# New order lists for an attention and LoRA block on one core, and the small vectors on SyncE's queue

## What is computed

```python
x = x + attn(layernorm(x))      # 32 query heads, 8 key/value heads of 128, q and k rms-normed, ALiBi, causal
x = x + ffn(layernorm(x))       # 8 LoRA experts of rank 16, all used, weighted by a softmax router
# attn: q, k, v = x@Wq.T, x@Wk.T, x@Wv.T;  out = softmax(q k^T/sqrt(128) + bias) v;  out @ Wo.T
# ffn:  2 * sum_h 8*softmax(x@Wr.T + br)_h * (x @ A_h.T) @ B_h.T
```

## Time and profile before

| | us |
|---|---|
| median of 3 runs | 2099.63 (2098.99 to 2102.61) |
| the profiled execution | 2102.15 |
| its span, first to last instruction | 2100.4 |
| PE busy in it | 2031.2 (97%) |
| DVE, ACT, POOL busy | 1364.3, 1149.8, 1113.1 |

### The profile page before, as it was taken

How to read it: one execution, slowest core, us unless ns; L and a number is a source line. 1 busy time by engine, 2 the same in 40 slices (tenths; PEclk the granted TensorE clock), 3 DMA queues, 4 the chain that set the end, 5 groups by cost and what they waited for, 6 DMA issues and landing times.

```text
span 2100.4 us, 33654 instructions
## 1 busy us (share of the span) xinstructions
PE 2031.2 (97%) x11196; PEld 1724.8 (82%) x11196; DVE 1364.3 (65%) x3431; ACT 1149.8 (55%) x3314; POOL 1113.1 (53%) x1128
## 2 busy tenths in 40 slices
PE   7999999999999999999999999999999999999996
PEld 6888888888888888887878788887888888787874
DVE  6657656566666666669765666565666656566785
ACT  4656546565555646655545455555555555555551
POOL 3554645546355554646645656454564645456462
PEclk9999999999999999999999999999999999999998
DMA  3573535636364463654544536354453635444342
GB/s 121 145 166 89 150 95 150 141 105 156 102 162 100 127 171 85 159 160 130 133 125 115 126 81 148 95 125 116 106 107 90 146 94 127 117 104 98 80 99 64
DMA packets 738699, 252.35 MB, mean 120 GB/s; under 512 B 551000, under 2 KB 682072, under 8 KB 738528
## 3 DMA queue, kind: packets, MB, share of 16 engines
q1 hardware_dynamic: 686192, 147.96, 33.4%
q10 hardware_dynamic: 52336, 102.25, 14.1%
HBM read 136.86 MB, written 113.25 MB: 119 GB/s over the span
## 4 chain that ended last, share of the span: by engine, by line
PE 87%; DVE 5%; ACT 2%; POOL 2%; issue 2%; DMA 1%; SPq 0%; ACTq 0%; DVEq 0%; POOLq 0%
PE s_ps L1047 18%; PE o_ps L1047 17%; PE y_ps L1047 16%; PE q_ps L1047 15%; PE turn_ps L1134 11%; PE turn_ps L1047 8%; POOL pT_lo L826 1%; DVE oT_lo L970 1%; ACT pT_hi L735 1%; ACT oT_hi L762 1%; PE turn_ps L1128 1%; DVE pT_lo L919 1%; DMA p_raw<-p_bounce 0%; DVE qn L953 0%; SPq L589 0%
## 5 line engine op out<-in xcount | busy, mean ns | idle before, releaser
L826 POOL TENSOR_TENSOR pT_lo<-p_raw,pT_hi 128x512 fp32r<-128x512 f32 x256 | 331.1, 1300 | 243.2 <-ACT pT_hi L735 242.7
L820 POOL TENSOR_TENSOR probs_odd<-probs_odd,p_inv 128x256 f32<-128x256 f32 (+3 forms) x256 | 316.5, 1256 | 186.1 <-DVE p_inv L949 185.9
L820 POOL TENSOR_TENSOR probs_even<-probs_even,p_inv 128x128 f32<-128x128 f32 (+3 forms) x256 | 261.1, 1042 | 196.6 <-DVE p_inv L949 195.6
L735 ACT ACTIVATE pT_hi<-p_raw 128x512 fp32r<-128x512 f32 x256 | 161.4, 631 | 238.3 <-PE o_ps L1047 132.5
L919 DVE TENSOR_TENSOR pT_lo<-turn_ps,pT_hi 128x512 fp32r<-128x512 f32 x320 | 218.1, 684 | 93.8 <-ACT pT_hi L727 92.4
L1047 PE MATMUL s_ps<-kT_hi,qT_hi 128*128 128x512 f32 (+3 forms) x768 | 273.2, 356 | 3.5 <-DVE neg_max L942 2.2
L942 DVE CUSTOM_DVE_ANT_0 probs_odd<-s_ps,rel 128x256 f32<-128x256 f32 (+3 forms) x256 | 209.0, 820 | 98.9 <-issue 97.6
L727 ACT ACTIVATE pT_hi<-turn_ps 128x512 fp32r<-128x512 f32 x320 | 188.8, 596 | 150.5 <-PE turn_ps L1134 148.8
L1047 PE MATMUL s_ps<-kT_hi,qT_lo 128*128 128x512 f32 (+3 forms) x768 | 262.3, 341 | 0.0
L1047 PE MATMUL s_ps<-kT_lo,qT_hi 128*128 128x512 f32 (+3 forms) x768 | 261.4, 340 | 0.0
L1047 PE MATMUL o_ps<-pT_hi,v_hi 128*128 128x512 f32 x576 | 244.2, 424 | 13.7 <-POOL pT_lo L826 8.1
(11 more groups left out here) (110 smaller groups left out, 4614.3 us busy)
## 6 DMA issues: line engine op xcount, KB each, us to landing
p_raw<-p_bounce SPq DMA_DIRECT2D x1024, 64.0 KB, 2.3
p_bounce<-probs_odd SPq DMA_DIRECT2D x64, 320.0 KB, 2.8
p_bounce<-probs_odd SPq DMA_DIRECT2D x64, 192.0 KB, 4.2
p_bounce<-probs_even SPq DMA_DIRECT2D x64, 192.0 KB, 2.1
wq_kept<-wqT_hi ACTq DMA_DIRECT2D x8, 1024.0 KB, 4.4
wq_kept<-wqT_lo ACTq DMA_DIRECT2D x8, 1024.0 KB, 6.8
p_bounce<-probs_odd SPq DMA_DIRECT2D x64, 128.0 KB, 1.8
p_bounce<-probs_even SPq DMA_DIRECT2D x64, 128.0 KB, 1.8
```

Source lines behind the costliest of these rows:

```text
L735: nc.scalar.activation(pT_hi[:, p_slot[w, s, j], :], p_raw[:, fetch_number[w, s, j] % RAW_TILES, :], ACT.Copy).then_inc(sems["upper_p"], 1)
L820: nc.gpsimd.tensor_tensor(row, row, p_inv[:, s % 2, h:h + 1].to_broadcast((P, L)), ALU.mult).then_inc(sems["normalise"], 1)
L826: nc.gpsimd.tensor_tensor(pT_lo[:, r, :], p_raw[:, fetch_number[w, s, j] % RAW_TILES, :], pT_hi[:, r, :].bitcast(F32), ALU.subtract).then_ ...
```

## The change

The three small loads are taken from the front of ACT's program and put into SP's, in `load_wo.first`, ahead of its wait. Every string has a new order; each has exactly the items that it had (125, 498, 666, 503, 465 and 569). The tables `MEMORY_TILES`, `MEMORY_SLOTS` and `RAW_TILES` can now differ from batch to batch, but both batches have the values of before; the counting of slots and raw tiles starts anew with the second batch.

```diff
-MEMORY_TILES = {2: (2,), 3: (2, 3), 4: (3, 4), 5: (3, 4, 5), 6: (4, 5, 6), 7: (3, 4, 5, 6, 7)}
+MEMORY_TILES = ({2: (2,), 3: (2, 3), 4: (3, 4), 5: (3, 4, 5), 6: (4, 5, 6), 7: (3, 4, 5, 6, 7)},
+                {2: (2,), 3: (2, 3), 4: (3, 4), 5: (3, 4, 5), 6: (4, 5, 6), 7: (3, 4, 5, 6, 7)})
-    TURN_SLOTS, MEMORY_SLOTS, RAW_TILES = 2, 2, 3
+    TURN_SLOTS = 2
+    MEMORY_SLOTS, RAW_TILES = (2, 2), (3, 3)
 @@ block.sync, load_wo(w, *first)
+                    sp.dma_start(wk_norm[:], k_norm_w.rearrange("(p a) -> p a", a=1)).then_inc(small_loaded, 16)
+                    sp.dma_start(wq_norm[:], q_norm_w.rearrange("(p a) -> p a", a=1)).then_inc(small_loaded, 16)
+                    sp.dma_start(br_row[:], br.rearrange("(a n) -> a n", a=1).broadcast_to((P, NE))).then_inc(small_loaded, 16)
                     after(sp, "turn", "wq", 0, C - 1)
                     sp.dma_start(w_raw[:, 0:G, :], wo_v[0]).then_inc(wo_loaded, 16)
 @@ block.scalar
-            act.dma_start(wk_norm[:], k_norm_w.rearrange("(p a) -> p a", a=1)).then_inc(small_loaded, 16)
-            act.dma_start(wq_norm[:], q_norm_w.rearrange("(p a) -> p a", a=1)).then_inc(small_loaded, 16)
-            act.dma_start(br_row[:], br.rearrange("(a n) -> a n", a=1).broadcast_to((P, NE))).then_inc(small_loaded, 16)
```

The strings, cut to the parts that the text below speaks of. PROLOGUE (its head; what follows has a new order too):

```diff
-"load_y.0 load_y.4 load_wq.first x_stats.0 x_moments.0 x_stats.4 load_y.3 x_moments.4 load_y.2 x_rstd.4 load_y.7 "
-"x_rstd.0 x_norm.4 load_y.1 x_norm.0 turn.wq.0 load_y.5 turn.wq.1 x_stats.3 high.wq.0 turn.wq.2 load_wkv.first "
+"load_y.0 load_y.1 load_y.4 load_wkv.first x_stats.0 load_y.3 x_moments.0 x_stats.1 x_rstd.0 load_y.5 x_moments.1 "
+"x_stats.4 load_wq.first x_rstd.1 x_norm.1 turn.wkv.0 x_norm.0 high.wkv.0 x_stats.3 turn.x.0 x_stats.5 turn.x.1 "
+"load_y.7 high.x.0 x_moments.4 low.wkv.0 high.x.1 x_rstd.4 load_y.2 x_moments.3 low.x.0 x_rstd.3 turn.wkv.1 "
+"load_y.6 low.x.1 high.wkv.1 x_moments.5 x_norm.3 turn.wq.0 low.wkv.1 turn.wq.1 high.wq.0 high.wq.1 low.wq.0 "
+"turn.wq.2 low.wq.1 high.wq.2 turn.wq.3 x_stats.2 turn.kv.0 high.wq.3 load_wo.first low.wq.2 x_moments.2 low.wq.3 "
```

More of the change, by code:

```diff
@@ L330, in attention_lora_block, with through_memory, values_order @@
         plans.setdefault(w, group_a if w < NG else group_b)
-    def through_memory(s):
-        return list(MEMORY_TILES.get(s, ()))
-    def values_order(s):
-        return [j for j in range(s + 1) if j not in through_memory(s)] + through_memory(s)
+    def through_memory(w, s):
+        return list(MEMORY_TILES[w // NG].get(s, ()))
+    def values_order(w, s):
+        return [j for j in range(s + 1) if j not in through_memory(w, s)] + through_memory(w, s)
     def ffn_batch(w):
@@ L484, in attention_lora_block, with p_high, p_low, raw_p @@
         b_sorted = f_x[:, 1, :].rearrange("p (o h r) -> p o h r", o=C, r=RK)
+        def p_high(slot):
+            more = slot - TURN_SLOTS - MEMORY_SLOTS[0]
+            return pT_hi[:, slot, :] if more < 0 else w_raw[:, 2 * more, :].bitcast(F32R)
+        def p_low(slot):
+            more = slot - TURN_SLOTS - MEMORY_SLOTS[0]
+            return pT_lo[:, slot, :] if more < 0 else w_raw[:, 2 * more + 1, :].bitcast(F32R)
+        def raw_p(n):
+            return p_raw[:, n, :] if n < RAW_TILES[0] else w_raw[:, G + n - RAW_TILES[0], :]
         def x_source(b, t):
@@ L571, in send_p @@
             def send_p(w, s, h):
-                first = through_memory(s)[0]
+                first = through_memory(w, s)[0]
                 before = [name for name in sent if name[1] % 2 == s % 2 and sent[name] == sent[w, s] - 16 * G]
                 if before and h == 0:
-                    after(sp, "flip_p", *before[0], through_memory(before[0][1])[-1])
+                    after(sp, "flip_p", *before[0], through_memory(*before[0])[-1])
                 after(sp, "normalise", w, s, h)
@@ L896, in low @@
                     r = p_slot[w, *which]
-                    target, upper = pT_lo[:, r, :], pT_hi[:, r, :]
+                    target, upper = p_low(r), p_high(r)
                 elif of == "q":
```

66 lines of the change are left out of this document (36 added, 30 removed), and 512 rows, old and new, of tables (BOUNDARY, FIRST_B, GROUP_A, GROUP_B).

## The result

The changed kernel takes 2083.03 us in the median of four runs (2082.91 to 2086.43), the kernel before 2100.53 beside it (2098.99 to 2102.61). The ratio is 0.9915, with a 95% interval of 0.9902 to 0.9929. That is 17.5 us less, where 7.0 was forecast. Measured once more, the changed kernel took 2084.90 and the kernel before 2101.36 beside it, a ratio of 0.9919 (0.9905 to 0.9932). The traced execution of the changed kernel took 2086.43, 3.3 us more than its other three; none of those three has a trace.

What follows compares the result with a forecast made beforehand. PE, busy 97% of the span, bounds the kernel; only 69 us idle can go. Terms -1.5 -1.4 -1.0 -0.8 +0.9 -3.2 sum to -7.0; with the profiled run's offset to the median carried over, 2092.6 us, range 2085 to 2102.

Steps and rivals of the forecast that it cites:

- GROUP_A: Seven groups of the first batch: net -0.2 us a group, -1.4 in all, each off by 0.4 either way.
- GROUP_B: Six groups of the second batch: net +0.15 us a group, +0.9 in all, with +0.68 ahead of `y.7`.
- Prologue: Start of the kernel: PE starts at 7.5, Wq lands near 12; 1.5 us gained, bounds 3 gained to 1.5 lost.
- Rival (4): Small loads on SP's queue: moving them saves issue time only, prologue starts at 8.0, not 7.5; no chance of its own.
- so the first wait goes: End of a first-batch group: PE's 0.48 us wait for `lower_p.7.7` goes, as `q.9.2` adds 0.68 of work before `values.7.7`.
- BOUNDARY: Group between the batches: +0.7 at its start, -1.7 of its 4.7 idle by judgement; net -1 us, from -3 to +2.
- FIRST_B: First group of the second batch: `lower_p` waits go in large part, `y.6` being ahead of `values.7.6`; -0.8 us, -2.5 to +1.5.
- rival (1): Gains given back, 2100 us: a `low` or `max` moved behind a `flip_p` waits for its DMA; chance 0.25.
- LAST: Last group: +0.9 at its start, -0.6 in the middle, -3.5 at its end; net -3.2 us, from -7 to +3.
- a chain ... 18.05 us: Last group: from `y.6` through `add_y.6`, norm, `turn.f.6`, gates and `turn.lora.6` to `f_out.6`, 18.05 us.
- (2): Slower, 2106 us: `load_wkv` beside tile fetches makes `values.7.6` and `values.7.7` late by 1.9 in seven groups; chance 0.12.
- (3): Larger gain, 2087 us: the list's slack is better throughout, steady groups at -0.6 and -0.3 us each; chance 0.2.

Runs made afterwards that it cites:

- The joints: Kernel before, BOUNDARY in the new order only behind `y.3`, only up to `f_out.1`, or only up to `f_out.3`: 2106.93, 2099.97 and 2097.60 us.

## Why the prediction was wrong

The direction was right. The size was not: the range's lower end was 2085, and the kernel took 2083. The terms of GROUP_A and GROUP_B came out within 0.5 us, the first of them by luck.

- **Bound and method.** PE's work stayed as it was and only idle time went, as said, but for some half-clock time. The step that failed in the method is "An order changes a stall in one way: by how much PE work lies between". An order also moves what stands in DVE's and POOL's queues: `norm_k` beside `lower_p.7.7`, `o_low.6` behind a flip, the fetches of FIRST_B 2.4 us late. The chain's length is then no constant that can be taken over.
- **Prologue.** Right in its path (start at 7.4, Wq near 12, gain small against the earlier start). The start of 7.5 was right in part by luck: it took 1 us off for the small loads, and the kernel that moved them alone started at 8.85, against 9.0 to 10.0 with the old order. The two traces give 1.6 against 1.5; over all traces it is 2.7. The second group is 1 to 2 us shorter behind it, and no step of the sum had that. Rival (4), as to the small vectors, is borne out by the run that moved them alone.
- **GROUP_A.** The forecast wanted 125.7 for a steady group, and no wait for `pT_lo` ahead of `values.7.7`. It mostly came out at 126.3, with that wait at 0.67. The step that failed is "so the first wait goes": the work between was counted, the length of `lower_p.7.7` was taken as fixed. It grew by 1.0 beside `norm_k`, which the new string puts there. The stall of 0.3 ahead of `scores.1.2` did not come. The seven groups still won 1.9, near the forecast's 1.4 by luck, because the wait of the earlier trace rows went, which the forecast had as a rival's danger and not as a gain.
- **GROUP_B.** Right: 123.3 to 123.4 against 123.4, and `y.7` 1.57 us late behind `values.7.7`.
- **BOUNDARY.** The term was -1.0 and measured -5.1. The step that failed is the one called a judgement, "-1.7 of its 4.7 idle". It took its idle time from PE's busy column (149.13 less 144.41). The column hides a part of the waits. Start to start, item by item, the waits of this group summed to 9.8 us in before and 4.3 after (how much is counted in each depends on the distances taken as free of a wait; the difference is that of the stretch, 5.5). The joints show that they add up one by one. At the start `turn.q.1` has no wait in the new order, where +0.7 was counted, and a wait of 0.65 ahead of `scores.1.0` went.
- **FIRST_B.** -0.8 forecast, +1.1 measured, +1.5 at full clock. The priced wait ahead of `values.7.7` did go (1.61 to 0.68 start to start), but others decided. `values.7.0` was not looked at, and it waits 1.9 us for `o_low.6` behind a flip whose fetch was issued 2.4 us later. That is near rival (1)'s mechanism, "moved behind a `flip_p` waits for its DMA"; moving it back did not help, as the fetch was still late.
- **LAST.** -3.2 forecast, -8.7 measured. The part from `f_out.6` to `y.7` was right in its number, 5.53 to 2.27, -3.3 against -3.5, but 1.3 of it is clock: the same old order takes 4.22 at full clock. The step that failed is "a chain ... 18.05 us", taken over whole. From `y.6` to `f_out.6` it is now 14.7 us (2048.89 to 2063.57). Its first part, `y.6` to `turn.f.6`, is 7.3 in both. The part behind it fell from 10.7 to 7.4, 1.5 of that by the clock and 1.8 by the order. "Denser work can only raise it" was written, and no number given to it: it is 2.8 us. The head, at +0.3 in the sum, gave -2.4.
- **The rivals.** (1) is true of FIRST_B, in that its gain is eaten up, and of a head of LAST without its tail, not of the whole. (2) is refuted: load and fetch did not collide. (3) named the size nearest to the result, but by other means: the steady groups gave nothing of it. The chance of a faster kernel adds up to 0.55 and was given as 0.6.

What stays open: what decides in which execution the clock falls at the end of the old FIRST_B; whether `load_wkv`'s place counts; what makes POOL late in the new FIRST_B; and where three of the changed kernel's four executions were 3.3 us shorter than the traced one. Fewer groups with the long `lower_p.7.7` would do it, but no trace of them shows it.
